# First layer's node scores in a four-layer graph network: the turned nodes as stationary operand, six score columns streaming

## What is computed

```python
hW = h @ W                                          # 2708x256
hp = (node_adj > 0).astype(hW.dtype) @ hW
hm = (node_adj < 0).astype(hW.dtype) @ hW
e_plus = leaky_relu(concatenate([hp, hm], axis=1) @ a, 0.2)[:, 0]
e_minus = leaky_relu(concatenate([hm, hp], axis=1) @ a, 0.2)[:, 0]
```

## Time and profile before

| | us |
|---|---|
| median of three runs | 2114.61 |
| lowest and highest | 2113.03, 2115.75 |
| the profiled execution, whole | 2117.71 |
| its span, first to last instruction | 2116.0 |
| PE busy in it | 2046.6 (97%) |
| nodes' turning, scores and turning back, from the first transposition to the first of stage A | 11.66 to 30.68 |

### The profile page before, as it was taken

The page is one execution under the profiler, slowest core; times in us unless marked ns, Lnnn a source line. Parts: engine busy times, 40 slices in busy tenths (PEclk is TensorE's granted clock), DMA queues, the critical chain, the costliest instruction groups (busy, mean ns, idle before and its releaser), DMA issues.

```text
span 2116.0 us, 28365 instructions
## 1 busy us (share of the span) xinstructions
PE 2046.6 (97%) x10838; PEld 1156.1 (55%) x10847; DVE 1526.1 (72%) x2511; ACT 970.4 (46%) x1517; POOL 89.7 (4%) x113
## 2 busy tenths in 40 slices
PE   7999998799999998999999999999999999999997
PEld 4555665344444454555555544455899985333343
DVE  4665556798988877544578894344589987999988
ACT  3222224698988878755222220000411326654555
POOL 0000000000000000000000010000000102000000
PEclk9999999899999999999999999999999999999999
DMA  7665654355564554654000015444100004333331
GB/s 237 210 210 190 199 182 178 143 205 191 179 227 168 198 184 144 224 172 135 20 0 1 0 35 135 131 127 110 54 1 2 1 1 182 115 87 110 84 88 56
DMA packets 124647, 260.14 MB, mean 123 GB/s; under 512 B 14643, under 2 KB 54121, under 8 KB 121929
## 3 DMA queue, kind: packets, MB, share of 16 engines
q1 hardware_dynamic: 106185, 228.95, 34.0%
q10 hardware_dynamic: 18324, 29.34, 3.7%
HBM read 217.66 MB, written 40.59 MB: 122 GB/s over the span
## 4 chain that ended last, share of the span: by engine, by line
PE 72%; DVE 17%; ACT 6%; issue 2%; DMA 1%; POOL 0%; SPq 0%; DVEq 0%; ACTq 0%
PE banks L1083 21%; PE banks L1136 10%; PE banks L1170 9%; PE banks L986 9%; PE banks L1215 8%; PE banks L1234 4%; PE banks L975 3%; DVE arena L2300 3%; DVE arena L1832 2%; ACT arena L1361 2%; PE banks L889 2%; PE banks L1027 2%; DVE arena L1913 1%; DVE arena L2016 1%; DVE arena L2017 1%
## 5 line engine op out<-in xcount | busy, mean ns | idle before, releaser
L1083 PE MATMUL banks<-arena 128*128 128x512 f32 (+2 forms) x1512 | 583.2, 544 | 17.3 <-DVE arena L1913 17.2
L1083 PEld LDWEIGHTS banks<-arena 128*128 128x128 f32 x1512 | 282.8, 190 | 308.3 <-issue 229.1
L1913 DVE TENSOR_TENSOR arena<-arena 128x1536 f32<-128x1536 f32 (+4 forms) x132 | 201.9, 1529 | 150.2 <-ACT arena L1397 134.3
L2300 DVE SCALAR_TENSOR_TENSOR arena<-arena 128x1024 f32<-128x1024 f32 (+3 forms) x264 | 288.3, 1165 | 10.2 <-PE banks L1234 9.2
L1170 PE MATMUL banks<-arena 128*128 128x129 f32 (+1 forms) x1936 | 221.2, 276 | 3.5 <-DVE arena L2199 3.1
L986 PE MATMUL banks<-arena 128*128 128x512 f32 (+4 forms) x528 | 223.8, 545 | 0.2 <-ACT arena L1302 0.2
L1170 PEld LDWEIGHTS banks<-arena 128*128 128x128 f32 (+1 forms) x1936 | 217.8, 192 | 7.1 <-DVE arena L2199 3.8
L1215 PE MATMUL banks<-arena 128*32 128x512 f32 (+1 forms) x2112 | 215.5, 545 | 3.0 <-DVE arena L2300 3.0
L1136 PE MATMUL banks<-arena 128*128 128x512 f32 (+4 forms) x528 | 206.0, 544 | 1.2 <-DVE arena L2008 1.2
L1832 DVE CUSTOM_DVE_ANT_0 arena<-arena 128x2708 f32<-128x2708 bf16 (+1 forms) x66 | 196.2, 2973 | 2.2 <-DMA arena<-e_rows 1.9
L1397 ACT ACTIVATE arena<-arena 128x1536 f32<-128x1536 f32 (+4 forms) x132 | 170.6, 1292 | 57.3 <-DVE arena L1895 57.0
(11 more groups left out here) (245 smaller groups left out, 2197.1 us busy)
## 6 DMA issues: line engine op xcount, KB each, us to landing
arena<-hw_rows SPq DMA_DIRECT2D x126, 384.0 KB, 3.1
arena<-adj_T SPq DMA_DIRECT2D x126, 256.0 KB, 3.3
arena<-in_adj SPq DMA_DIRECT2D x17, 1354.0 KB
arena<-in_adj SPq DMA_DIRECT2D x42, 512.0 KB
adj_T<-arena ACTq DMA_DIRECT2D x63, 256.0 KB, 2.2
arena<-adj_T SPq DMA_DIRECT2D x84, 192.0 KB, 2.9
arena<-in_adj SPq DMA_DIRECT2D x15, 1024.0 KB
arena<-in_adj SPq DMA_DIRECT2D x15, 768.0 KB
```

Source lines behind the costliest of these rows:

```text
L1083: ins = PE.matmul(bank(2 * (c % 2) + f)[:, 0:wid(c)], hs[0:R, m % 3, h * D + f * P:h * D + (f + 1) * P], weights_of(n)[0:R, h, 0:wid(c)], ...
L1913: V.tensor_tensor(e, e, a, ALU.mult).then_inc(s["p_ok"], 1)
L2300: V.scalar_tensor_tensor(PM3[0:k, n % 3, h, 0:w], r3_bc[0:k, h, c * WW:c * WW + w], smalls[0:k, 4, h * T + t:h * T + t + 1], mask3[0:k, n ...
```

## The change

The product is done the other way round. The turned nodes of a tile (128 features by up to 128 nodes) become the stationary operand, and the six columns of `wa0` stream. What comes out is nodes by six scores, which is what DVE wants, so it goes straight into bank 5. The rows `u_rows`, ACT's six copies, the semaphore `u_sb` and the 22 transpositions back are gone; there are now 44 products (22 tiles, two halves of the features) instead of 12. They stand between the turnings: from the fifth pair on, behind each `x_turned(g)` comes `x_scored(g - 4)`, and the last four pairs are scored at the end. The wait for `scores_ok` moves with the first of them. `u_mm` is counted once.

```diff
+SCORED_BEHIND = 4
-            def x_scored(c):
-                lo, hi = c * W, min(N, c * W + W)
-                pe.wait_ge(projs[0][1], min(PAIRS, 2 * (c + 1)))
-                if c >= 2:
-                    pe.wait_ge(u_sb, c - 1)
-                for kk in range(KD):
-                    ins = PE.matmul(bank(c % 2)[0:2 * H0, 0:hi - lo], wa0[:, kk, :], supT[:, kk, lo:hi], start=kk == 0, stop=kk == KD - 1)
-                ins.then_inc(u_mm, 1)
+            def x_scored(g):
+                if g == 0:
+                    pe.wait_ge(scores_ok, 1)
+                pe.wait_ge(projs[0][1], g + 1)
+                for t in (2 * g, 2 * g + 1):
+                    for kk in range(KD):
+                        ins = PE.matmul(bank(5)[0:kp(t), t * 2 * H0:(t + 1) * 2 * H0], supT[:, kk, t * R:t * R + kp(t)], wa0[:, kk, :],
+                                        start=kk == 0, stop=kk == KD - 1)
+                return ins
             for g in range(PAIRS):
                 x_turned(g)
-            pe.wait_ge(scores_ok, 1)
-            for c in range(-(-N // W)):
-                x_scored(c)
-            for t in range(T):
-                pe.wait_ge(u_sb, t // RPC + 1)
-                ins = PE.transpose(bank(5)[0:kp(t), t * 2 * H0:(t + 1) * 2 * H0], u_rows[:, t * R:t * R + kp(t)], ident[0:2 * H0, 0:2 * H0])
+                if g >= SCORED_BEHIND:
+                    x_scored(g - SCORED_BEHIND)
+            for g in range(PAIRS - SCORED_BEHIND, PAIRS):
+                ins = x_scored(g)
             ins.then_inc(u_mm, 1)
...
-            for c in range(-(-N // W)):
-                lo, hi = c * W, min(N, c * W + W)
-                act.wait_ge(u_mm, c + 1)
-                S.copy(u_rows[:, lo:hi], bank(c % 2)[0:2 * H0, 0:hi - lo]).then_inc(u_sb, 1)
...
-            dve.wait_ge(u_mm, -(-N // W) + 1)
+            dve.wait_ge(u_mm, 1)
```

More of the change, by code:

```diff
@@ L305, in build @@
         srow = sb(2, N)
-        u_rows = srow[0:2 * H0, 0, :]
         first_at = top[0]
@@ L397, in build @@
         w0_in, late_in = sem("w0_in"), sem("late_in")
-        u_mm, u_sb = sem("u_mm"), sem("u_sb")
+        u_mm = sem("u_mm")
         hw_first, hw_second = sem("hw_first"), sem("hw_second")
```

## The result

| | median us | lowest, highest | runs |
|---|---|---|---|
| before | 2116.86 | 2113.03, 2123.63 | 13 |
| changed | 2120.75 | 2117.92, 2126.47 | 13 |

The ratio is 1.0021, with a 95% interval of 1.0011 to 1.0031: the changed kernel is slower, by 2.3 to 6.6 us. The three runs of before known ahead of the prediction had a median of 2114.61; with ten more it is 2116.86. The ratios and intervals, here and in the experiments, are those on record; they are not the quotients of the two medians beside them. The profiled execution of the changed kernel took 2125.84 us, with a span of 2124.1.

The account below looks back on a forecast made before the run. PE, busy 97% of the span, was taken as the bound; -2.4 (full clock) + 6.8 (half-clock scores) + 0.9 (stage A's first unit) = +5.3 on 2114.6 gave 2119.9 us, likeliest case 2116.0 to 2124.0, whole range 2111.0 to 2123.5.

Parts of the forecast that it names:

- Removed work: Score matmuls and turning back, 20.08 us to stage A's first transposition at 30.68: 10.60 us, all on the path.
- Price of a load: In the 44 new products, 84 full loads at 0.1125 us plus four small ones: 9.6 us added.
- The lower bound: For the new products' loads, 0.065 us each as in the turning back, 5.6 us in all.
- the rival of cheap loads: New score loads as cheap as in the turning back, clock stays: 5.6 us for 9.6, total 2108.2; chance 0.04.
- Sum at full clock: Last score ends at 28.3 us, so stage A starts 2.4 us earlier if TensorE's clock stays where it was.
- Where the clock is lost: Within the mixed turnings and scores, clock falls to half at 21.5 us, bracketed 18.3 to 28: +6.8 us; chance 0.58.
- a last possibility: Clock not yet risen when the scores begin may not rise before stage A: +10 us possible.
- First unit of stage A at half clock: Its transpositions and matmuls take 5.4 us instead of 2.7; DVE's 4.25 us chain hides all but 1.1; taken as +0.9.
- The rival that the clock stays: In the scores, PE loading and streaming without a gap keeps its clock whatever it streams: 2112.2 us; chance 0.31.
- Switching: Rival: 13 switches between turnings and products at up to 0.2 us each, 2.6 us, eat the gain: 2114.8; chance 0.04.

Follow-up runs that it names:

- the run with the scores behind: Changed kernel with the six-column products placed behind all turnings instead of between them; 2122.49 us, ratio 1.0029 to the kernel before.
- the one with 126 columns: Changed kernel with the six columns streamed 21 times in a row, results in six PSUM banks, no warming; 2114.57 us, ratio 0.9990 to before.
- 60 columns, not warmed: Changed kernel with the six columns streamed ten times per product, no zero matmuls ahead; 2115.50 us against 2116.46, ratio 0.9993.
- the warmed kernel: Changed kernel, still six columns, with 34 matmuls of zeros ahead of the nodes' landing; 2120.98 us, ratio 1.0019 to before.

## Why the prediction was right, and where it was not

The direction and the cause were right. The forecast was 2119.9 us, +5.3 on the median then known; measured were 2120.75, +3.9 (2.3 to 6.6) on that of 13 runs. That the two times lie only 0.9 us apart is luck: the loss was taken 1.4 us too large, and the median it was added to stood 2.3 us lower than that of 13 runs. The loss is even a little under the 4.2 us that the prediction called the least to be told from no change; with 13 runs of each kernel the interval excludes none all the same. The step on which it rested, that PE can be full and still lose its clock when little streams, is shown by the run with the scores behind (a fall after 2.1 us of loads, with PE full) and by the one with 126 columns (the loss is gone).

- **Removed work**, 10.6 us on the path: right. The versions that keep the clock have a section 2.3 us below before (60 columns, not warmed) with it gone.
- **Price of a load**: taken as 0.1125 us from L1170; it is 0.112, with 6, 60 and 126 columns streaming. The doubt whether the 129 columns at L1170 hid something was unfounded. The lower bound, 0.065 from the turning back, was out, and the rival of cheap loads with it.
- **Sum at full clock**, -2.4 us: the section of the 60-column kernel is -2.3. The terms agree too: from the first score to the end of the last PE works for 12.5 us (15.85 to 28.39) where 12.6 was forecast. The clock rose 0.4 us later after the first turning in this profile than in that of before, but the 20 turnings ahead of the scores took the same time (4.24 and 4.22 us).
- **Where the clock is lost**: the placement at 21.5 us has no profile for it. In both profiles of the changed kernel the clock had not risen at all by the end of the scores. I had named the missing rise as a last possibility, at +10 us, and that is what their sections show: 33.3 and 33.2 against 23.3. By the mean clocks above this was so in five of 21 executions. In the other 16 the clock seems to have risen and fallen again, as the sum supposed, and their median lies about 3 us above before, in place of 5.3. When it fell in them is not known; in the warmed kernel the mixture carried the clock for 7.8 us, to 23.0, so a later fall than at 21.5 is the likelier reason why the loss is smaller, but that is not shown.
- **First unit of stage A at half clock**, +0.9 us beyond DVE's cover: from the last score to the first mask product it is 5.7 us (40.08 to 45.75) in place of 4.2, so +1.5. The clock came back later in the unit than assumed. With the scores behind, where it was back at 39.1 us, the same distance is 4.35 us (36.24 to 40.59), so almost nothing was lost there.
- **The rival that the clock stays** (2112.2) named its mechanism rightly enough to be refuted: a PE that loads without a gap did not keep its clock. The Trainium skill ("TensorE: Matmul & The Clock Gate", "Why this matters for your kernels") asks for a TensorE kept busy and for no long idle gap; here, with 16.7 to 40.0 us free of gaps, the trace doesn't agree. With 60 or 126 columns it does.
- **Switching** cost nothing that can be seen: 1.33 us is a turning plus eight loads.

## What to carry to other kernels

Making the small operand stream and the large one stationary turns a product into a row of weight loads, and in these runs such a row, with six columns streaming past each load, neither raised TensorE's clock nor held it up: PE was full and ran at 1.2 GHz. Where such a stretch is a few microseconds long, look at the durations of like instructions in it and next to it, not at busy shares. Here streaming the same six columns ten times, hidden behind each load, cost nothing and took the time from 0.2% above the kernel before to no worse than it. Warming the clock with zeros ahead of the data shortened the section by 1.0 us (22.3 against 23.3, 20.0 against 21.0), which the whole time can't confirm; 26 zero matmuls together with 60 columns are clear of before, by 0.14% (0.9977 to 0.9995).

## What the runs showed of the hardware

- Matmuls of zeros raise the clock: 34 of them, from 2.9 us on, brought it up at 6.0 to 8.7 us, before the first turning; without them it rose at 14.9 us at the earliest.
- float32 loads of 128x128 in a product follow each other 0.112 us apart at full clock and 0.213 at half clock, with six streaming columns; at full clock it is the same with 60 and 126. The 22 loads of the turning back (6 rows by 128 columns) followed each other about 0.065 us apart.
- The mixture of turnings and six-column scores carried a clock that came in at 1.00 for 7.8 us and then lost it (one profile), and did not raise one that came in at 0.50, over 15 us (two profiles).
- The clock column begins with the first recorded change; ahead of it 1.00 is printed whatever it was. The changed kernel's first 45 us show it.
- The landing of the same nodes varies between profiles by 1.5 us or so, and the 2080 us behind the section by 4 us, which is why a microsecond is hard to see in this kernel even with five rounds.
